# Two-layer graph network: turned 32 x 32 blocks exchanged from SBUF to SBUF by sixteen transfers, in place of four stores and a load

## Chip, cores and metric

One NeuronCore of a Trainium2 chip. The metric is the device time of one execution in microseconds, as the median of several runs. Engines are named PE (TensorE), DVE (VectorE), ACT (ScalarE), POOL (GpSimd) and SP (SyncE, which issues most of the DMA transfers); PEld is TensorE's weight load.

## What is computed

50,000 nodes with 256 channels, 12,500 edges. Cut to what matters:

```
h   = relu(layernorm(x))                             # per node
agg = zeros.at[dst].add(relu(h[src] + edge_attr))    # 12,500 edges
g   = (h + agg) @ W1 + b1                            # 256 -> 512
g   = (g - mean) / sqrt(var + eps) * gamma + beta    # over all nodes
y   = relu(g) @ W2 + b2                              # 512 -> 256
x1  = x + h + relu(graph_norms(y))                   # statistics over all nodes
out = x1 + relu(h1 @ W + segment_sum((h1 @ M)[src])) # h1 = relu(layernorm(x1))
```

The change lies in the two matrix products with W1 and W2, which the kernel calls its stage 2.

## The kernel before

The kernel has four stages, each a block of programs for the five engines with semaphores between them. Stage 1 reads x and the edges, and gathers the statistics for the batch norm. Stage 2 forms h + agg, multiplies by W1 and W2 and writes y and x + h to the table `xy_table` in DRAM. Stages 3 and 4 do the graph norms, the second layer, and its edges.

Stage 2 works on groups of 512 nodes: 128 partitions of 4 nodes (`T`), 97 whole groups and a last one of 84 partitions, 98 (`NG`) in all. A group k passes through these steps, each on one engine, each group one step behind the group before:

- SP loads x (`load_rows`, L1011), POOL gathers the sums of the edges into `ar` (`gather`, L1072), ACT forms h in `hr` (`norm`, L1099), DVE adds them in `ar` (`add`, L1196).
- The product needs channels on the partitions, so `ar` (nodes on the partitions) must be transposed. For groups 0, 1 and 97 (`by_tensor`, L919) TensorE does it. For the other 95 groups DVE transposes inside 32 x 32 blocks (`turn_blocks`, L1214) into `blocks`, the memory of `W2s`, which no longer holds a weight. Then the blocks themselves must change places across the partitions: a quadrant q of 32 source partitions (`SQ`, `QUADS` = 4) holds, for each half c of the channels and each destination quadrant b, a run of 128 numbers.
- That exchange goes through a DRAM table `ht_table`: SP stores each source quadrant to it (`store_blocks`, L1037: four transfers of 128 KB), and when all four have landed loads the whole, 512 KB, into `staged` (`load_turned`, L1001), which is the memory of `WM` for even groups and of `W1s` for odd ones.
- ACT rounds the turned group to `tH` (`keep_high`, L1148), DVE takes the rest as `tL` (`keep_low`, L1224). TensorE multiplies W1 in two parts with `tH`, `tL` (`hidden`, L1346: 4 x 6 matmuls), ACT applies batch norm and relu into `r`, ACT and DVE split that into `rH` and `rL`, and TensorE multiplies W2 (`output`, L1360: 4 x 6 matmuls). ACT keeps y (`keep_y`, L1134), DVE takes statistics, SP stores y (`store_y`, L1029) and x + h (`store_rows`, L1021; called xh below).

The order on every engine is written out by hand: a `step(k)` for ACT, DVE and TensorE, a loop for SP. SP's loop (L1056) calls, for each k, `load_turned(k + 2)`, `load_rows(k + 5)`, `store_rows(k + 2)`, `store_y(k - 2)`, `clear_slots(k - 1)`, `store_blocks(k + 3)`, each with its wait in front; SP executes them in this order, and what waits holds up what follows. `load_rows` reuses the buffer of four groups before (`NU` = 4), so it waits until the xh store of that group has landed. `blocks` is a single buffer: DVE's `turn_blocks(k)` waits until the four stores of group k - 1 have landed (L1220), and `store_blocks` waits for the turn. `staged` has two buffers, free when `tL` of the group two before is made. The first eight groups (`KEPT`) stay in SBUF and have no xh and y stores.

Of the kernel before, what the change touches and what calls it, by code (L numbers as in the profile page):

```python
# [5 lines left out]
FP32 = mybir.dt.float32  # L6
# [6 lines left out]
P = 128  # L13
# [7 lines left out]
KC = CH // P  # L21
# [9 lines left out]
SQ = 32  # L31
QUADS = P // SQ
# [18 lines left out]
def is_int(k):  # L51
    return isinstance(k, int)
# [7 lines left out]
def after(eng, sem, count):  # L60

    if not is_int(count) or count > 0:
        eng.wait_ge(sem, count)


def group_shape(k):

    return (LAST, T) if is_int(k) and k == NG - 1 else (P, T)


def columns(k):

    p, n = group_shape(k)
    return p * n


def group_rows(table, k):

    return table[bass.ds(k * GC, columns(k)), :].rearrange("(p t) c -> p t c", t=T)


def group_block(table, k):

    return table[k] if is_int(k) else table[bass.ds(k, 1)].rearrange("a p b n -> (a p) b n")


def xh_part(block):

    return block[:, 0, :].rearrange("p (t c) -> p t c", t=T)


def y_part(block):

    return block[:, 1, :].rearrange("p (c n) -> p c n", c=KC)
# [51 lines left out]
def gnn_kernel(nc, x, src, dst, edge_attr, W1, b1, bn_gamma, bn_beta, W2, b2, ln_w, ln_b,  # L146
# [9 lines left out]
    xy_table = nc.dram_tensor("xy_table", (NG, P, 2, T * CH), FP32, kind="Internal").ap()  # L156
    x1_table = nc.dram_tensor("x1_table", (NODES, CH), FP32, kind="Internal").ap()
    x1d_table = nc.dram_tensor("x1d_table", (ET * P, CH), FP32, kind="Internal").ap()
    ht_table = nc.dram_tensor("ht_table", (2, QUADS, SQ, KC, QUADS, P), FP32, kind="Internal").ap()

    with ExitStack() as ctx:
        def sb(name, shape, dt=FP32, scope=ctx, side="left"):
# [7 lines left out]
        def sem(name):  # L170
            phase.append(nc.alloc_semaphore(name))
            return phase[-1]
# [740 lines left out]
        def stays(k):  # L913
            return is_int(k) and k < KEPT

        def exists(k):
            return 0 <= k < NG

        def by_tensor(k):  # L919

            return k in (0, 1, NG - 1)

        def turns_until(k):

            return {0: 1, 1: 2, NG - 1: 3}[k]

        def blocks_until(k):

            return k - 1

        def exchanges(k):

            return k // 2

        blocks = W2s[:].rearrange("p a b -> p (a b)")
        staged = [WM[:].rearrange("p a b c -> p (a b c)"), W1s[:].rearrange("p a b -> p (a b)")]
# [9 lines left out]
        xh2_done = sem("xh2_done")  # L946
        h2_done = sem("h2_done")
        blocks_made = sem("blocks_made")
        ht_out = [sem(f"ht_out{s}") for s in range(2)]
        ht_in = [sem(f"ht_in{s}") for s in range(2)]  # L950
        t2_made = sem("t2_made")
        th_kept = sem("th_kept")
# [13 lines left out]
        with ExitStack() as scope, nc.Block() as block:  # L966
# [14 lines left out]
            def xbuf(k):  # L981

                return xh_part(xy_kept[:, k, :, :]) if stays(k) else xr[:, k % NU, :, :]

            def ybuf(k):
                return y_part(xy_kept[:, k, :, :]) if stays(k) else yr[:, k % AU, :, :]

            def turned_part(k, c, n):

                if by_tensor(k):  # L990
                    return hT_ps[:, c, 0:n]
                return staged[k % 2][:, c * GC:(c + 1) * GC].rearrange("p (q t n) -> p t q n", q=QUADS, t=T)

            def nodes_of(part, k):

                return part if by_tensor(k) else part.rearrange("p (t q n) -> p t q n", q=QUADS, t=T)

            @block.sync
            def _(sp):

                def load_turned(k):  # L1001
                    if not exists(k) or by_tensor(k):
                        return
                    if k == 3:
                        sp.wait_ge(q_made, 1)
                    sp.wait_ge(ht_out[k % 2], 16 * QUADS * exchanges(k))
                    after(sp, tl_kept, k - 1)
                    sp.dma_start(staged[k % 2], ht_table[k % 2].rearrange("b p c q n -> (b p) (c q n)")
                                 ).then_inc(ht_in[k % 2], 16)

                def load_rows(k):  # L1011
                    if not exists(k):
                        return
                    p, n = group_shape(k)
                    if k < KEPT + NU:
                        after(sp, h2n_done, k - NU + 1)
                    else:
                        sp.wait_ge(xh_out[k % NU], 16 * (k // NU - KEPT // NU))
                    sp.dma_start(xbuf(k)[0:p, 0:n, :], group_rows(x, k)).then_inc(x2_in[k % NU], 16)

                def store_rows(k):  # L1021
                    if not exists(k) or stays(k):
                        return
                    p, n = group_shape(k)
                    sp.wait_ge(xh2_done, k + 1)
                    sp.dma_start(xh_part(group_block(xy_table, k))[0:p, 0:n, :],
                                 xbuf(k)[0:p, 0:n, :]).then_inc(xh_out[k % NU], 16)

                def store_y(k):  # L1029
                    if not exists(k) or stays(k):  # L1030
                        return
                    n = columns(k)
                    sp.wait_ge(y_kept, k + 1)
                    sp.dma_start(y_part(group_block(xy_table, k))[:, :, 0:n],
                                 ybuf(k)[:, :, 0:n]).then_inc(y_out[k % AU], 16)

                def store_blocks(k):  # L1037
                    if not exists(k) or by_tensor(k):
                        return
                    sp.wait_ge(blocks_made, blocks_until(k))  # L1040
                    after(sp, ht_in[k % 2], 16 * (exchanges(k) - 1))
                    for q in range(QUADS):
                        sp.dma_start(ht_table[k % 2, :, :, :, q, :].rearrange("b p c n -> p c b n"),
                                     blocks[q * SQ:(q + 1) * SQ, :].rearrange("p (c b n) -> p c b n", c=KC, b=QUADS)
                                     ).then_inc(ht_out[k % 2], 16)

                def clear_slots(t):
                    if not 0 <= t < ET:
                        return
                    if t == 0:  # L1050
                        sp.wait_ge(blank_made, 1)
                    sp.dma_start(x1d_table[t * P:(t + 1) * P, :], blank[:]).then_inc(slots_clear, 16)

                for k in range(3):
                    load_rows(k)
                for k in range(-2, NG + 3):  # L1056
                    load_turned(k + 2)
                    load_rows(k + 5)
                    store_rows(k + 2)
                    store_y(k - 2)  # L1060
                    clear_slots(k - 1)
                    store_blocks(k + 3)
                sp.wait_ge(slots_clear, 16 * ET)
                for s in range(AU):
                    sp.wait_ge(y_out[s], 16 * (-(-(NG - s) // AU) - KEPT // AU))
                for s in range(NU):
                    sp.wait_ge(xh_out[s], 16 * (-(-(NG - s) // NU) - KEPT // NU))
# [30 lines left out]
            def _(act):  # L1098
# [49 lines left out]
                def keep_high(k):  # L1148
                    if not exists(k):
                        return  # L1150
                    n = columns(k)
                    if by_tensor(k):
                        act.wait_ge(t2_made, turns_until(k))
                    else:
                        act.wait_ge(ht_in[k % 2], 16 * exchanges(k))
                    after(act, z_made, (k - 1) * HC)
                    for c in range(KC):
                        last = act.activation(nodes_of(tH[:, k % 2, c, 0:n], k), turned_part(k, c, n), ACT.Copy)
                    last.then_inc(th_kept, 1)
# [25 lines left out]
                act.wait_ge(var_made, 1)  # L1185
                act.activation(small[:, 4, :], small[:, 3, :], ACT.Sqrt, bias=eps[:]).then_inc(sdev_made, 1)
                keep_high(0)
                for piece in norm(2):
                    piece()
# [5 lines left out]
            def _(dve):  # L1195
# [18 lines left out]
                def turn_blocks(k):  # L1214

                    if not exists(k) or by_tensor(k):
                        return
                    dve.wait_ge(h2_done, k + 1)
                    if k > 2:
                        dve.wait_ge(ht_out[(k - 1) % 2], 16 * QUADS * exchanges(k - 1))  # L1220
                    dve.transpose(blocks.rearrange("p (b t n) -> p t b n", b=KC * QUADS, t=T),  # L1221
                                  ar[:, k % AU, :, :].rearrange("p t (b n) -> p t b n", n=SQ)).then_inc(blocks_made, 1)

# [99 lines left out]
                residual(2)  # L1323
                add(2)
                turn_blocks(2)
                for k in range(NG + 2):
                    step(k)
# [770 lines left out]
```

## Time and profile before

| | |
|---|---|
| runs | 2348.55 us median of 3 (2345.96 to 2351.61) |
| profiled execution | 2350.93 us, its span 2349.2 us |
| PE busy in the span | 2269.6 us (97%) |
| DVE busy | 1953.0 us (83%) |
| ACT busy | 1832.8 us (78%) |
| POOL busy | 1399.4 us (60%) |
| stage 2 | about 460 to 1545 us of the span |
| queue of the transfers that SP issues | 559.53 MB, 69.4% of 16 DMA engines' time |

The span runs from the first to the last instruction of the one execution that the profiler recorded. Busy time says how long an engine was at work, not that it set the pace; that is read stage by stage, from what waits for what. TensorE's matmuls overlap in the record, so their durations add up to more than the time they take; the number of matmuls in a stretch is the better measure of pace. A line number (L1043) is that of the listing above.

### The profile page before, as it was taken

To read this page: it belongs to the slowest core of one execution; us is meant where nothing else is said; L and a number is where in the kernel's file an instruction comes from. 1 tells how busy PE (TensorE), PEld (TensorE's weight loads), DVE (VectorE), ACT (ScalarE), POOL (GpSimd) and SP (SyncE) were. 2 spreads that over 40 slices of the span, in tenths; PEclk is the share of its full clock that TensorE was granted. 3 is DMA by queue.
4 is the path that set the end of the run, shared out by engine and by line. 5 is a ranking of instruction groups with operands and counts; after the bars stand their busy time and mean duration, and the time that the engine had idled before them with its cause. 6 is when DMAs were issued, how large, how long until landed. Compare 5 with 4: busy or idle time off the path is not lost. (4 is left out here: it accounts for less than half of the span.)

```text
span 2349.2 us, 45141 instructions
## 1 busy us (share of the span) xinstructions
PE 2269.6 (97%) x11499; PEld 1933.4 (82%) x11499; DVE 1953.0 (83%) x5704; ACT 1832.8 (78%) x3645; POOL 1399.4 (60%) x1403
## 2 busy tenths in 40 slices
PE   7999999699999999999999999979999999999997
PEld 6888888478888888788888788859988888989997
DVE  8999998488888888888888888767777777779996
ACT  6999999477777777877777877758888888866664
POOL 5777777464444444445444444237777777777775
PEclk8999999799999999999999999989999999999999
DMA  7899897367878888878877888679999999775662
GB/s 251 279 278 280 271 281 216 105 196 216 255 253 262 262 259 249 269 249 268 260 246 255 268 252 259 214 293 402 410 412 412 414 412 410 298 235 162 172 178 99
DMA packets 360084, 632.17 MB, mean 269 GB/s; under 512 B 61456, under 2 KB 246057, under 8 KB 348482
## 3 DMA queue, kind: packets, MB, share of 16 engines
q1 hardware_dynamic: 300018, 559.53, 69.4%
q0 software_dynamic: 59808, 70.24, 10.3%
q8 instruction: 81, 1.33, 0.2%
q14 instruction: 129, 1.06, 0.1%
q10 hardware_dynamic: 48, 0.01, 0.0%
HBM read 390.04 MB, written 336.65 MB: 309 GB/s over the span
## 5 line engine op out<-in xcount | busy, mean ns | idle before, releaser
L1087 POOL DMA_INDIRECT ar<-sum_table,ids x392 | 409.7, 1045 | 177.9 <-issue 96.2
L1655 POOL DMA_INDIRECT x1d_table<-x1r,slot x392 | 382.5, 976 | 141.7 <-issue 126.1
L1123 ACT ACTIVATE r<-pair,bnC,bnA 128x512 f32<-128x512 f32 x392 | 302.2, 771 | 90.6 <-PE pair L1356 80.0
L2021 PE MATMUL pair<-WM,h1T 128*128 128x256 f32 x1568 | 358.9, 382 | 3.9 <-DVE orr L1847 3.1
L2021 PEld LDWEIGHTS pair<-WM,h1T 128*128 128x128 f32 x1568 | 289.5, 189 | 49.2 <-issue 10.5
L1083 POOL MEMSET ar<- 128x1024 f32 x98 | 93.9, 958 | 386.9 <-DVE W2s L1221 366.2
L835 PE MATMUL bank<-hr 128*128 128x257 f32 (+1 forms) x1568 | 274.3, 329 | 9.3 <-ACT hr L536 9.2
L835 PEld LDWEIGHTS bank<-hr 128*128 128x128 f32 x1568 | 250.9, 192 | 36.8 <-ACT hr L536 9.9
L1268 DVE TENSOR_TENSOR rL<-r,rH 128x512 fp32r<-128x512 f32 x392 | 265.9, 679 | 11.3 <-ACT rH L1132 3.7
L1356 PE MATMUL pair<-tH,W1h 128*128 128x512 f32 (+1 forms) x784 | 242.8, 391 | 8.4 <-DVE tL L1230 8.4
L1356 PE MATMUL pair<-tH,W1l 128*128 128x512 f32 (+1 forms) x784 | 241.8, 390 | 0.0
L1356 PE MATMUL pair<-tL,W1h 128*128 128x512 f32 (+1 forms) x784 | 241.5, 389 | 0.0
L1847 DVE SCALAR_TENSOR_TENSOR orr<-pair,x1r 128x1024 f32<-128x1024 f32 x98 | 120.0, 1225 | 130.6 <-DMA out<-orr 84.5
L1736 ACT ACTIVATE h1r<-x1r,n,r 128x256 f32<-128x256 f32 x392 | 202.6, 593 | 0.0
L536 ACT ACTIVATE hr<-xr,nmr,rstd 128x256 f32<-128x256 f32 x392 | 202.4, 587 | 0.3 <-PE bank L835 0.2
L1109 ACT ACTIVATE hr<-xr,nmr,rstd 128x256 f32<-128x256 f32 x360 | 194.7, 589 | 0.0
L1356 PEld LDWEIGHTS pair<-tH,W1h 128*128 128x128 f32 x784 | 146.9, 188 | 41.8 <-DVE tL L1230 11.7
L1356 PEld LDWEIGHTS pair<-tL,W1h 128*128 128x128 f32 x784 | 147.6, 188 | 30.6
L1356 PEld LDWEIGHTS pair<-tH,W1l 128*128 128x128 f32 x784 | 147.6, 188 | 30.6
L1257 DVE CAST rH<-r 128x512 fp32r<-128x512 f32 x196 | 84.3, 430 | 102.0 <-ACT r L1123 101.8
L1221 DVE STREAM_TRANSPOSE W2s<-ar 128x1024 f32<-128x1024 f32 x95 | 118.3, 1245 | 51.8 <-DMA ht_table<-W2s 50.6
L1372 PE MATMUL pair<-rH,W2h 128*128 128x512 f32 x392 | 153.0, 390 | 0.0
(254 smaller groups left out, 5723.7 us busy)
## 6 DMA issues: line engine op xcount, KB each, us to landing
xr<-in_x SPq DMA_DIRECT2D x186, 512.0 KB, 5.9
xy_kept<-xy_table SPq DMA_DIRECT2D x57, 1024.0 KB, 20.5
x_table<-x1r SPq DMA_DIRECT2D x97, 512.0 KB, 19.9
out<-orr SPq DMA_DIRECT2D x97, 512.0 KB
ht_table<-W2s SPq DMA_DIRECT2D x380, 128.0 KB
xy_table<-xr SPq DMA_DIRECT2D x89, 512.0 KB, 6.6
xy_table<-yr SPq DMA_DIRECT2D x89, 512.0 KB, 7.5
xyr<-xy_table SPq DMA_DIRECT2D x32, 1024.0 KB, 20.1
```

The costliest lines, as they stand in the source:

```text
L536: last = act.activation(hr[0:p, h, j, 0:CH], xr[0:p, s, j, :], ACT.Relu, bias=nmr[0:p, bass.ds(k * T + j, 1)], scale=rstd[0:p, bass.ds(k * ...
L835: return pe.matmul(o, a, b, start=False, stop=False, skip_group_check=True)
L1087: pool.indirect_dma_start(ar[0:p, s, j, :], None, sum_table[:, :], bass.IndirectOffsetOnAxis(ap=ids[0:p, k * T + j:k * T + j + 1], axis=0) ...
L1109: one = act.activation(hr[0:p, k % AU, j, :], xbuf(k)[0:p, j, :], ACT.Relu, bias=nmr[0:p, k * T + j:k * T + j + 1], scale=rstd[0:p, k * T ...
L1123: act.activation(r32[:, m, 0:n], z_ps[m][:, 0:n], ACT.Relu, bias=bnC[:, m:m + 1], scale=bnA[:, m:m + 1]).then_inc(r_kept, 1)
L1268: dve.tensor_tensor(rL[:, k % 2, m, 0:n], r32[:, m, 0:n], rH[:, k % 2, m, 0:n].bitcast(FP32), ALU.subtract).then_inc(rl_kept, 1)
L1356: last = pe.matmul(z_ps[m][:, 0:n], w[:, c, m * P:(m + 1) * P], t[:, k % 2, c, 0:n], start=i == 0, stop=i == len(parts) - 1)
L1372: last = pe.matmul(y_ps[k % 2][c][:, 0:n], w[:, m, c * P:(c + 1) * P], t[:, k % 2, m, 0:n], start=m == 0 and i == 0, stop=m == HC - 1 and ...
L1655: pool.indirect_dma_start(x1d_table[:, :], bass.IndirectOffsetOnAxis(ap=slot[0:p, part, s * T + j:s * T + j + 1], axis=0), x1r[0:p, s, j, ...
L1736: last = act.activation(h1r[0:p, f, j, :], x1r[0:p, s, j, :], ACT.Relu, bias=n3[0:p, s, j:j + 1], scale=r3[0:p, s, j:j + 1])
L1847: dve.scalar_tensor_tensor(out=flat(orr[:, s, :, :], p, n), in0=flat(u_pair(k)[:, :, :], p, n), scalar=0.0, in1=flat(x1r[:, b, :, :], p, n ...
L2021: last = pe.matmul(tile_of(u_pair(k), j)[0:p, :], h1T[:, s, c, j * p:j * p + p], Ws[:, c, :], start=c == 0, stop=c == KC - 1)
```

## The change

The table `ht_table` and its semaphores `ht_out` go. `load_turned` and `store_blocks` are replaced by `exchange`, sixteen transfers from `blocks` to `staged`: for each source quadrant q and destination quadrant b, 32 partitions x 2 runs of 128 numbers, 32 KB. The waits are those of the functions that it replaces: the turn must be made, and `staged` free. ACT's `keep_high` and DVE's `turn_blocks` wait for all sixteen. In SP's loop `load_rows(k + 5)` now stands first.

```
-                def load_turned(k):
+                def exchange(k):
                     if not exists(k) or by_tensor(k):
                         return
-                    if k == 3:
+                    if exchanges(k) == 1:
                         sp.wait_ge(q_made, 1)
-                    sp.wait_ge(ht_out[k % 2], 16 * QUADS * exchanges(k))
+                    sp.wait_ge(blocks_made, blocks_until(k))
                     after(sp, tl_kept, k - 1)
-                    sp.dma_start(staged[k % 2], ht_table[k % 2].rearrange("b p c q n -> (b p) (c q n)")
-                                 ).then_inc(ht_in[k % 2], 16)
+                    for q in range(QUADS):
+                        here = blocks[q * SQ:(q + 1) * SQ, :].rearrange("p (c b n) -> p c b n", c=KC, b=QUADS)
+                        for b in range(QUADS):
+                            there = staged[k % 2][b * SQ:(b + 1) * SQ, :].rearrange(
+                                "p (c q n) -> p c q n", c=KC, q=QUADS)
+                            sp.dma_start(there[:, :, q, :], here[:, :, b, :]).then_inc(ht_in[k % 2], 16)
...
-                def store_blocks(k):
-                    if not exists(k) or by_tensor(k):
-                        return
-                    sp.wait_ge(blocks_made, blocks_until(k))
-                    after(sp, ht_in[k % 2], 16 * (exchanges(k) - 1))
-                    for q in range(QUADS):
-                        sp.dma_start(ht_table[k % 2, :, :, :, q, :].rearrange("b p c n -> p c b n"),
-                                     blocks[q * SQ:(q + 1) * SQ, :].rearrange("p (c b n) -> p c b n", c=KC, b=QUADS)
-                                     ).then_inc(ht_out[k % 2], 16)
...
                 for k in range(-2, NG + 3):
-                    load_turned(k + 2)
                     load_rows(k + 5)
+                    exchange(k + 2)
                     store_rows(k + 2)
                     store_y(k - 2)
                     clear_slots(k - 1)
-                    store_blocks(k + 3)
...
-                        act.wait_ge(ht_in[k % 2], 16 * exchanges(k))
+                        act.wait_ge(ht_in[k % 2], 16 * QUADS * QUADS * exchanges(k))
...
-                        dve.wait_ge(ht_out[(k - 1) % 2], 16 * QUADS * exchanges(k - 1))
+                        dve.wait_ge(ht_in[(k - 1) % 2], 16 * QUADS * QUADS * exchanges(k - 1))
```

On SP, in the middle of stage 2, one round of the loop and the start of the next read so before (L1043 are the four stores, `W2s` is `blocks`; `WM` and `W1s` are the two `staged`; L1019 loads x, L1026 stores xh, L1034 stores y, L1052 clears rows of a table of stage 3):

```order
L1008 DMA WM<-ht_table 128x1024
L1019 DMA xr2<-in_x 128x1024
L1026 DMA xy_table<-xr2 128x1024
L1034 DMA xy_table<-yr 128x1024
L1052 DMA x1d_table<-blank 128x256
L1043 DMA ht_table<-W2s 64x4x128 x4
L1008 DMA W1s<-ht_table 128x1024
```

and so with the change (its lines are numbered anew: L1011 is the exchange, L1021 loads x, L1028 stores xh, L1036 stores y, L1044 clears):

```order
L1021 DMA xr2<-in_x 128x1024
L1011 DMA WM<-W2s 32x2x128 x16
L1028 DMA xy_table<-xr2 128x1024
L1036 DMA xy_table<-yr 128x1024
L1044 DMA x1d_table<-blank 128x256
L1021 DMA xr2<-in_x 128x1024
L1011 DMA W1s<-W2s 32x2x128 x16
```

The load from the table, which stood between the clear and the load of x, is gone, and the exchange stands between the load of x and the xh store. The other four engines have as many instructions as before, in the same order.

## Rows read from the trace of the kernel before

**Rows 1.** Windows of 100 us in stage 2; (x) is the number of instructions.

```profile
core 0: us, PE busy (x) PEld busy (x) DVE busy (x) ACT busy (x) POOL busy (x), PEclk, DMA share, GB/s
...
860.00:960.00 100.00, 98.62 (x434) 80.95 (x433) 82.62 (x116) 76.24 (x126) 45.40 (x45) 1.00 0.81 255
...
1060.00:1160.00 100.00, 100.00 (x443) 82.81 (x442) 85.02 (x120) 77.92 (x130) 47.93 (x47) 1.00 0.82 260
1160.00:1260.00 100.00, 99.32 (x437) 81.54 (x437) 83.29 (x117) 75.79 (x127) 45.71 (x46) 1.00 0.80 257
1260.00:1360.00 100.00, 98.06 (x433) 80.79 (x432) 84.41 (x119) 77.23 (x130) 46.79 (x47) 1.00 0.82 260
```

**Rows 2.** Waits, 470 to 1540 us: who waited for whom, us, times, longest.

```profile
ACT tH L1158 <- DMA WM<-ht_table: 54.5, 33, 4.4
DVE W2s L1221 <- DMA ht_table<-W2s: 50.6, 63, 2.5
ACT tH L1158 <- DMA W1s<-ht_table: 46.6, 30, 2.9
...
PE pair L1356 <- DVE tL L1230: 8.4, 6, 4.3
...
SPq L1008 <- DMA ht_table<-W2s: 371.3, 94, 6.8
```

**Rows 3.** One step in order of time: start, us, engine, line [idle before].

```profile
1001.40 0.33 SPq L1008 DMA_DIRECT2D WM<-ht_table  x1
1001.47 1.25 DVE L1221 STREAM_TRANSPOSE W2s<-ar 128x1024 f32<-128x1024 f32 x1 [1.81 <-DMA ht_table<-W2s]
1001.77 0.43 SPq L1019 DMA_DIRECT2D xr<-in_x  x1
1002.24 0.43 SPq L1026 DMA_DIRECT2D xy_table<-xr  x1
1002.72 0.43 SPq L1034 DMA_DIRECT2D xy_table<-yr  x1
...
1003.92 3.62 SPq L1043 DMA_DIRECT2D ht_table<-W2s  x4
...
1012.39 0.33 SPq L1008 DMA_DIRECT2D W1s<-ht_table  x1
1012.47 1.25 DVE L1221 STREAM_TRANSPOSE W2s<-ar 128x1024 f32<-128x1024 f32 x1 [0.71 <-DMA ht_table<-W2s]
...
1016.29 1.16 ACT L1158 ACTIVATE tH<-W1s 128x512 fp32r<-128x512 f32 x2 [1.81 <-DMA W1s<-ht_table]
```

**Rows 4.** Issues: four stores early, the stores of 560 to 1460 us, ACT's small loads.

```profile
478.40 2.55 SPq L1043 DMA_DIRECT2D ht_table<-W2s  x4
...
L1043 SPq DMA_DIRECT2D ht_table<-W2s x328: 575/869/2428, 562.6 to 1458.6; - x164
...
34.99 0.27 ACTq L590 DMA_DIRECT2D vec_rows<-in_L_gnn_ln_w  x1
35.30 0.28 ACTq L590 DMA_DIRECT2D vec_rows<-in_L_gnn_ln_b  x1
```

**Rows 5.** Issue and landing: a y store alone, then the xh stores of 560 to 1460.

```profile
L1034 SPq DMA_DIRECT2D xy_table<-yr x1: 319/319/319, 1517.1 to 1517.1; - x1
DMA to landing us min/median/max: 2.6/2.6/2.6
...
L1026 SPq DMA_DIRECT2D xy_table<-xr x81: 320/430/1412, 569.1 to 1452.6; - x81
DMA to landing us min/median/max: 5.8/6.6/7.4
```

**Rows 6.** The start of stage 2 in order of time.

```profile
470.19 2.70 SPq L1043 DMA_DIRECT2D ht_table<-W2s  x4
...
473.35 1.22 PE L1356 MATMUL pair<-tH,W1h 128*128 128x512 f32 x2 [4.29 <-DVE tL L1230]
...
475.24 0.33 SPq L1008 DMA_DIRECT2D WM<-ht_table  x1
```

More of the change, by code:

```diff
@@ L158, in gnn_kernel @@
     x1d_table = nc.dram_tensor("x1d_table", (ET * P, CH), FP32, kind="Internal").ap()
-    ht_table = nc.dram_tensor("ht_table", (2, QUADS, SQ, KC, QUADS, P), FP32, kind="Internal").ap()
     with ExitStack() as ctx:
@@ L948, in gnn_kernel @@
         blocks_made = sem("blocks_made")
-        ht_out = [sem(f"ht_out{s}") for s in range(2)]
         ht_in = [sem(f"ht_in{s}") for s in range(2)]
```

## Prediction

> **What bounds the kernel now.** I read the page first, then stage 2 (about 460 to 1545 us) in windows of 100 us, then the waits of that stage, then one step in order of time. The windows say who sets the pace: between 1060 and 1160 us TensorE is busy for 100.00 of 100 us and runs 443 matmuls [rows 1]. That is 100 / 443 = 0.2257 us a matmul; a group takes 48 of them (24 hidden, 24 output), so a step lasts 48 x 0.2257 = 10.83 us. VectorE (85.02) and ScalarE (77.92) have room in the same row. The page has 0.9 to 1.0 for TensorE's clock through these slices, so nothing is to be had there.
>
> What the table route costs is read from the windows that are not full: 434, 437 and 433 matmuls instead of 443 [rows 1], 9 + 6 + 10 = 25 too few, 25 x 0.2257 = 5.6 us. The waits name the cause: TensorE waits for `tL` [rows 2], which waits for `tH`, which waits for the load from the table (54.5 us for `WM` alone). The whole TensorE wait of the stage is 8.4 us [rows 2], but 4.29 us of it is one wait at 473 us [rows 6], for the `tL` of group 1, which TensorE turns and which never goes through the table.
>
> The other waits in rows 2 (VectorE 50.6 us for the stores, SyncE 371.3 us at the load) are off the path; the reader should see that they are nearly on it. In one step [rows 3] SyncE issues the load at 1001.40 and the next one at 1012.39: a round of 10.99 us, of which 1003.92 + 3.62 - 1001.40 = 6.14 us is issuing and 4.85 us is waiting for the stores to land. VectorE's next turn starts 0.08 us after that landing. So the route has a loop as long as TensorE's step, without reserve, and an unlucky transfer now and then makes TensorE wait.
>
> **What is removed and added.** Per group of the 95 that are exchanged, five issues (four stores, one load) go and sixteen come: SyncE goes from 9 to 20 issues a step, 1045 more in all. 512 KB written to DRAM and 512 KB read back become 512 KB from SBUF to SBUF, in 512-byte pieces as the stores had. No other engine gets another instruction. Two waits change: VectorE's turn waits for the exchange of the group before instead of its four stores, ScalarE's `tH` for the exchange instead of the load.
>
> **Price of one issue.** No row shows a 32 x 2 x 128 transfer. From below: small loads of a few rows on ScalarE's queue follow each other in 35.30 - 34.99 = 0.31 us [rows 4]. From above: the 128 KB stores, 2.55 / 4 = 0.64 us each with little ahead of them, and 0.87 us in the median of the full steps, where more stands in the queue [rows 4]. Between them stand the 128 x 1024 transfers, back to back 1002.24 - 1001.77 = 0.47 us [rows 3]. I take **0.40 us**: the new transfer has 64 pieces, between the few rows at 0.31 and the 128 rows at 0.47, and both sides have the same simple shape, unlike the stores. Sixteen: 6.4 us (5.0 at 0.31, 7.5 at 0.47, 10.2 at 0.64, 13.9 at 0.87). These are estimates from the rows named.
>
> **The loop on SyncE.** The new order is load x (k+5), exchange (k+2), store xh (k+2), store y, clear. The load of x waits until the store of xh of the step before has landed (the buffer of four steps ago). In the old order the wait for the stores stood between these two and hid the landing; now only the y store and the clear do. So a round is at least 0.47 (load of x) + 6.4 (exchange) + the landing of the xh store. Alone, a 512 KB store lands 2.6 us after its issue [rows 5]; in the old step the xh store takes 6.6 us, queued behind two 512 KB loads [rows 5]. In the new order it stands behind small transfers that come no faster than they are issued, so I take 3.1 us, near the lower end. Sum: 0.47 + 6.4 + 3.1 = **10.0 us**, 0.8 us inside the step of 10.83. Bounds: 0.47 + 5.0 + 2.6 = 8.1 and 0.47 + 13.9 + 6.6 = 21.0; I stay near the lower, since one 512 KB load stands ahead of the exchange and not the four transfers of rows 3.
>
> **The loop on VectorE.** Turn 1.25 us [rows 3], fifteen issues 6.0, the last transfer 2.0 to land (an estimate, below the 2.6 of a 512 KB store), 0.1 for signals: 9.4 us, also inside the step. The four 128 KB stores show that transfers overlap: issued from 470.19, all landed by 475.24 [rows 6], 5.05 us, not four times 2.6.
>
> **What that does to the chain.** Old: turn ends at 1001.47 + 1.25 = 1002.72, `tH` of that group starts at 1016.29 [rows 3], 13.6 us. New: 6.0 + 2.0 + 0.1 = 8.1 us after the turn. The 5.5 us saved become cushion before TensorE, so the 5.6 us of holes in rows 1 should close. If that cushion is gone, the holes come back. VectorE's 50.6 us and ScalarE's 101 us of waits go too, and turn into waiting for TensorE: nothing is gained there. At the start, the second exchange waits longer than its stores did (8 us against 5.05), so the turns of groups 3 and 4 come 1 to 2 us later; of TensorE's six waits for `tL` [rows 2] the one at 473 us is the only one in the start, and it comes before any exchange has landed, so I cost this at nothing; the step in hand between a turn and its use covers it. Stages 1, 3 and 4 are untouched.
>
> **Sum.** The profiled execution took 2350.93 us (span 2349.2 and 1.7 around it): 2350.93 - 5.6 = 2345.3. It is 2.4 us above the median of the three runs, 2348.55; part of the holes may be this execution's own, so against the median the gain is 2 to 5.6 us. I forecast **2345 us**, -0.15%, below the 0.2% (4.7 us) that a measurement of this kernel can tell from no change. Its own range: 2340 to 2349.
>
> **A rule that speaks against it.** The rows: 128 KB stores are issued 0.64 us apart, and the few-row loads 0.31 [rows 4], so a quarter of the bytes costs more than a quarter of the time: sixteen issues at 0.40 take 6.4 us where four take 2.55. The Trainium skill, "SBUF — State Buffer", section "The DMA setup-cost knee", asks for 128 partitions and the largest single transfer, since each pays a roughly fixed 2 us; sixteen in turn would be an estimated 32 us by that figure, three steps. Rows 6 disagree with the serial reading, since the four stores overlap. What the rows leave of it is the price of an issue, in rivals 1 and 2.
>
> **Rivals.**
> 1. *SyncE becomes the bound* (slower). Place: the wait of load x for the xh store. It decides as soon as sixteen issues and the landing exceed 10.83 - 0.47 = 10.36 us. With 0.47 us an issue and 3.1 us landing the round is 0.47 + 7.5 + 3.1 = 11.1, 0.25 us over; some 88 rounds have both (groups from 8 on store xh), +22 us: about 2370. With 0.50 us and 3.1 it is 11.6, +68 us, about 2415. For it: the reserve of 0.8 us is smaller than the step from 0.40 to 0.47 us an issue makes, 1.1 us. Against: 64 pieces a transfer are fewer than any 0.47 row has. Chance 25%.
> 2. *A small transfer holds the queue as long as a large one.* At the store's 0.64 us: 0.47 + 10.2 + 3.1 = 13.8, 3.0 us over, x 88 = +264 us, about 2610. Were they even to land in turn, 2.6 us each as in rows 5, a round would be 42 us and the stage nearly 3 ms longer, but rows 6 show four that overlap. Against: the 0.31 us row. Chance 7%, of which 1 for the serial case.
> 3. *The holes stay.* If TensorE's three holes come from slow stretches of the DMA engines that hit the exchange as well, nothing moves: 2348.5. Against: rows 2 tie them to the loads, and the route gains 5.5 us of cushion. Chance 8%.
>
> **How the numbers follow.** Forecast 60%, rivals 25, 7 and 8%. Of the forecast's 60%, some 25 points lie at 2344 and below (faster by over 0.2%), 35 within. Rival 3 (8) is within, and about 5 points of rival 1 (an overshoot under 0.05 us a round). Faster 25%, same 48%, slower 27%. For 8 in 10 the range takes the forecast, rival 3 and rival 1 up to 0.3 us over a round (0.3 x 88 = 26 us): 2340 to 2375. Left out are rival 2, the dearer part of rival 1, and a gain beyond 8.5 us, for which rows 1 have no room.
>
> **What the profile will show.** Right: no TensorE wait for `tL` between 560 and 1460 us and 443 matmuls in each full window; sixteen issues in 6 to 7 us; the wait of the turn for the exchange near zero; SyncE waiting for the turn, not for the xh store; DMA share down from about 0.8. Wrong, rival 1: SyncE's largest wait stands at the load of x, for the xh store's landing, and windows of 100 us hold fewer than 440 matmuls throughout. Rival 2: the issues are 0.6 us or more. A faster time than 2340 would mean that TensorE's 0.2257 us itself depended on the transfers.

## The result, and the profile after

The changed kernel takes **2621.11 us**, the median of three runs (2619.4 to 2623.92), against 2348.55: a ratio of 1.1155, 95% interval 1.1138 to 1.1172. It is slower by some 272 us. Forecast were 2345 us, with a range to 2375.

The changed kernel's page: the span, the busy time of the engines, and the queue of the transfers that SP issues.

```profile
span 2619.4 us, 46093 instructions
PE 2356.1 (90%) x11499; PEld 1949.0 (74%) x11499; DVE 1938.8 (74%) x5704; ACT 1830.5 (70%) x3645; POOL 1415.4 (54%) x1403
q1 hardware_dynamic: 304578, 509.79, 55.0%
```

The queue moves 50 MB less and its share falls from 69.4 to 55.0%, as the change meant it to. No engine has a larger share of the span for it. Windows of 100 us, with the columns of [rows 1]:

```profile
960.00:1060.00 100.00, 87.36 (x349) 67.77 (x349) 63.96 (x91) 60.38 (x100) 36.55 (x35) 0.95 0.50 165
1060.00:1160.00 100.00, 83.00 (x348) 63.80 (x347) 66.08 (x94) 61.41 (x103) 37.29 (x36) 1.00 0.52 173
...
1260.00:1360.00 100.00, 82.69 (x346) 63.40 (x344) 66.99 (x97) 61.72 (x103) 40.23 (x38) 1.00 0.51 166
```

These windows have 346 to 349 matmuls where [rows 1] had 433 to 443, and all twelve from 560 to 1760 us lie between 340 and 354. So this is no matter of single holes: 48 x 100 / 348 = 13.8 us a step, in all of stage 2. The same is read from VectorE's turns, whose line gives the start of the first and the last of 95 (first of the kernel before, then of the change):

```profile
L1221 DVE STREAM_TRANSPOSE W2s<-ar x95: 1245/1245/1248, 468.9 to 1494.6; 128x1024 f32<-128x1024 f32 x95
```

```profile
L1212 DVE STREAM_TRANSPOSE W2s<-ar x95: 1245/1245/1248, 468.5 to 1769.2; 128x1024 f32<-128x1024 f32 x95
```

The distance grew from 1025.7 to 1300.7 us, by 275 us: the whole loss lies between these two turns. Divided by 94 it is a mean round of 10.91 us before and 13.84 us after. I use this mean round for the experiments too.

What takes 13.8 us is seen in SP's issues in order of time (start, us, line), with VectorE's two turns beside them:

```profile
1004.95 1.25 DVE L1212 STREAM_TRANSPOSE W2s<-ar 128x1024 f32<-128x1024 f32 x1 [4.32 <-DMA WM<-W2s]
1006.51 0.33 SPq L1021 DMA_DIRECT2D xr<-in_x  x1
1006.94 10.18 SPq L1011 DMA_DIRECT2D W1s<-W2s  x16
1017.17 0.58 SPq L1028 DMA_DIRECT2D xy_table<-xr  x1
...
1018.52 1.25 DVE L1212 STREAM_TRANSPOSE W2s<-ar 128x1024 f32<-128x1024 f32 x1 [4.37 <-DMA W1s<-W2s]
1020.02 0.33 SPq L1021 DMA_DIRECT2D xr<-in_x  x1
```

From one load of x to the next are 13.51 us: 0.43 to the first issue of the exchange, 10.23 for the sixteen (10.18 and a gap), and 1020.02 - 1017.17 = 2.85 us from the xh store to the next load of x, which waits for its landing. Most of the 2.85 us goes on issuing the xh store, the y store and the clear; the wait that is left is 93.5 / 86 = 1.1 us a round (SP's line among the waits below). Each of the sixteen takes 10.23 / 16 = **0.64 us**. The lines of the exchange (into `W1s`; that into `WM` is alike) and of the xh store (min/median/max ns of an issue, first and last start) and the landing of the latter:

```profile
L1011 SPq DMA_DIRECT2D W1s<-W2s x752: 585/597/1934, 483.1 to 1767.2; - x188
...
L1028 SPq DMA_DIRECT2D xy_table<-xr x90: 575/584/1412, 560.0 to 1782.6; - x90
...
DMA to landing us min/median/max: 2.8/2.9/3.7
```

An issue lasts 597 ns in the median and follows the one before by some 40 ns more; a few take up to 1.9 us, which brings the mean round from 13.51 to 13.84. Last the waits of the stage, and SP's own:

```profile
DVE W2s L1212 <- DMA W1s<-W2s: 221.6, 47, 6.0
DVE W2s L1212 <- DMA WM<-W2s: 216.1, 47, 5.8
PE pair L1347 <- DVE tL L1221: 157.6, 95, 4.1
ACT tH L1149 <- DMA W1s<-W2s: 112.5, 47, 3.6
...
SPq L1021 <- DMA xy_table<-xr: 93.5, 86, 1.8
```

Against [rows 2] TensorE now waits for `tL` at each of the 95 groups (157.6 us where it was 8.4), the turn waits 437.7 us in all for the exchange, and SP's largest wait stands at the load of x: the place that the prediction named for rival 1, with the price of rival 2.

### The profile page after: what moved, and what is told of

Its sections match the earlier page's. It is cut to its first block and busy times, and to the rows that moved or that the text cites. A ratio compares the mean times of both kernels' runs of the same rounds, so it can differ in the third digit from the quotient of the medians.

```text
span 2619.4 us, 46093 instructions
## 1 busy us (share of the span) xinstructions
PE 2356.1 (90%) x11499; PEld 1949.0 (74%) x11499; DVE 1938.8 (74%) x5704; ACT 1830.5 (70%) x3645; POOL 1415.4 (54%) x1403
## 5 line engine op out<-in xcount | busy, mean ns | idle before, releaser
L1078 POOL DMA_INDIRECT ar<-sum_table,ids x392 | 427.4, 1090 | 177.9 <-issue 96.3
L1347 PE MATMUL pair<-tH,W1h 128*128 128x512 f32 (+1 forms) x784 | 257.1, 410 | 157.6 <-DVE tL L1221 157.6
L1347 PE MATMUL pair<-tL,W1h 128*128 128x512 f32 (+1 forms) x784 | 250.4, 402 | 0.0
L1347 PE MATMUL pair<-tH,W1l 128*128 128x512 f32 (+1 forms) x784 | 247.8, 398 | 0.0
L1363 PE MATMUL bank<-rH,W2h 128*128 128x512 f32 (+1 forms) x392 | 159.3, 406 | 24.5 <-DVE rL L1259 24.5
L1363 PE MATMUL pair<-rH,W2h 128*128 128x512 f32 x392 | 164.3, 419 | 13.1 <-DVE rL L1259 12.7
```

The lines of the kernel that those rows point to most:

```text
L1078: pool.indirect_dma_start(ar[0:p, s, j, :], None, sum_table[:, :], bass.IndirectOffsetOnAxis(ap=ids[0:p, k * T + j:k * T + j + 1], axis=0) ...
L1347: last = pe.matmul(z_ps[m][:, 0:n], w[:, c, m * P:(m + 1) * P], t[:, k % 2, c, 0:n], start=i == 0, stop=i == len(parts) - 1)
L1363: last = pe.matmul(y_ps[k % 2][c][:, 0:n], w[:, m, c * P:(c + 1) * P], t[:, k % 2, m, 0:n], start=m == 0 and i == 0, stop=m == HC - 1 and ...
```

## The experiments

Five of the kernels, e1, e2, e3, e5 and e11, were run once each. In e1, e2, e5 and e11 blocks land in other places or not at all: they serve to time transfers, and are no kernels to use. A ratio is taken to runs of the kernel before on the same chip, whose median is 2349.85 us for e1 to e4, 2351.6 for e5 to e7 and 2353.9 for e8 to e11.

### e1_shapes: is it the shape of the transfer?

The sixteen transfers of a group take nine shapes, by ranges of groups; two of them:

```
-                    for q in range(QUADS):
...
+                        elif k < 45:
+                            sp.dma_start(there[:, i * 64:i * 64 + 64],
+                                         blocks[:, i * 64:i * 64 + 64]).then_inc(inc, 16)
...
+                        elif k < 75:
+                            h, w = i % 8 * 16, i // 8 * 512
+                            sp.dma_start(there[h:h + 16, w:w + 512],
+                                         blocks[112 - h:128 - h, w:w + 512]).then_inc(inc, 16)
```

> The sixteen transfers of an exchange get nine shapes, each for some ten groups (31 to 13 in turn); the blocks land in other places or not at all, so the output is not the reference's. Shapes: 32x2x128 (as in the change), 32x256, 32x128 (half the bytes), 128x64, 128x2x32, 64x128, 16x512, 32x8x32, 128x32 (half the bytes). Theory 1, a price per issue: SyncE pays about 0.64 us for each, whatever it carries, in all nine; rounds of 13.5 us throughout. Theory 2, the bytes: the queue is held by moving 512-byte pieces from SBUF to SBUF, so the halved shapes 32x128 and 128x32 go down to about 0.32 us and their rounds to TensorE's 10.8 us, the rest stays at 0.64. Theory 3, the shape: transfers of 128 partitions cost 0.33 to 0.47 us as the 128x1024 ones do in the kernel before, those of 32 partitions 0.64; or the number of pieces decides, then 32x8x32 and 128x2x32 (256 pieces) are dearest and 16x512 cheapest.

It took 2622.25 us. Three of the nine lines of issues, in order 32 x 128 (half the bytes), 128 x 2 x 32 (four times the pieces) and 16 x 512:

```profile
L1017 SPq DMA_DIRECT2D W1s<-W2s x80: 512/591/1552, 785.9 to 904.8; - x80
...
L1023 SPq DMA_DIRECT2D W1s<-W2s x80: 600/621/1539, 1061.8 to 1186.7; - x80
...
L1031 SPq DMA_DIRECT2D W1s<-W2s x80: 507/589/1429, 1342.4 to 1462.5; - x80
```

All nine medians lie between 589 and 621 ns. From SBUF to SBUF, bytes (16 or 32 KB), pieces and partitions hardly matter: the price is one of the issue, and the time of the kernel does not move.

### e2_eight: half as many issues

Eight transfers of 64 partitions x 2 x 128 in place of sixteen of 32, with the same 512 KB in all:

```
+                    for i in range(8):
+                        h, w = i % 2 * 64, i // 2
+                        here = blocks[64 - h:128 - h, :].rearrange("p (c b n) -> p c b n", c=KC, b=QUADS)
+                        there = staged[k % 2][h:h + 64, :].rearrange("p (c q n) -> p c q n", c=KC, q=QUADS)
+                        sp.dma_start(there[:, :, w, :], here[:, :, w, :]).then_inc(ht_in[k % 2], 16)
```

> The same 512 KB in eight transfers of 64 partitions, 64x2x128, in place of sixteen of 32 (the blocks land in other places, so the output is not the reference's). Theory 1, a price per issue of 0.64 us: 8 x 0.64 = 5.1 us, a round of 0.47 + 5.1 + 2.9 = 8.5 us, below TensorE's 10.83, so the time is about 2345 us. Theory 2, the bytes: as many 512-byte pieces move, the exchange stays at 10.2 us and the time at 2620 us. Theory 3 with pieces or partitions in the price: between 0.64 and 1.28 us an issue; at 1.28 the time stays at 2620.

It took 2341.41 us, beside 2349.85 of the kernel before (median of 7, lowest 2344.18). One round of SP, and a window:

```profile
1006.14 5.14 SPq L1010 DMA_DIRECT2D WM<-W2s  x8
```

```profile
1260.00:1360.00 100.00, 100.00 (x443) 82.80 (x442) 85.16 (x119) 79.11 (x131) 46.10 (x47) 1.00 0.65 210
```

The price is the same, 5.14 / 8 = 0.64 us, and with eight of them the stage runs at TensorE's pace. So the number of issues makes the loss. The holes of [rows 1] are gone as well. This run changes SP's order along with the route, so it does not tell which of the two closes them; e9 below does.

### e3_load_after: the exchange ahead of the load of x

```
-                    load_rows(k + 5)
                     exchange(k + 2)
+                    load_rows(k + 5)
```

> The change with the load of x behind the exchange, so that SyncE no longer waits for the xh store between two exchanges. If the sixteen issues are the cost (theory 1), the next loop takes over, VectorE's: turn 1.25, signals 0.1, sixteen issues 10.2, landing 1.4: 13.0 us in place of 13.5, 88 x 0.5 = 44 us less, about 2577 us. If the order of the loop is the cost (the wait of the load of x for the xh store), the time falls to 2345 us.

2638.95 us, slower than the change. SP in order of time:

```profile
1011.11 10.97 SPq L1011 DMA_DIRECT2D W1s<-W2s  x16
1022.12 0.58 SPq L1021 DMA_DIRECT2D xr<-in_x  x1
...
1024.89 5.26 SPq L1011 DMA_DIRECT2D WM<-W2s  x7
```

The wait for the xh store is gone, and SP issues from end to end: 1024.89 - 1011.11 = 13.78 us, sixteen issues now 11.01 us (1022.12 - 1011.11). A round of 13.0 us was expected, VectorE's loop. It did not come, since the sixteen take 0.8 us more, most of it at their first, as a window that ends behind it shows; VectorE's turn of that round stands beside it:

```profile
1011.11 1.21 SPq L1011 DMA_DIRECT2D W1s<-W2s  x1
```

```profile
1023.46 1.25 DVE L1212 STREAM_TRANSPOSE W2s<-ar 128x1024 f32<-128x1024 f32 x1 [4.61 <-DMA W1s<-W2s]
```

VectorE's loop grows by the same time: its turn ends at 1023.46 + 1.25 = 1024.71, 0.18 us before the next exchange, so here the loops on SP and on VectorE are equally long. The order of the load of x alone is not the cost.

### e5_ends: does the price hang on the two ends?

The sixteen transfers go between other ends, by ranges of groups, by way of two tables in DRAM made for it (`probe`, strided, and `probe_flat`, one run of 32 KB a transfer):

```
+                        elif k < 35:
+                            sp.dma_start(there[b * SQ:(b + 1) * SQ, :].rearrange("p (c q n) -> p c q n", c=KC, q=QUADS)[:, :, q, :],
+                                         probe[k % 2, b, :, :, q, :]).then_inc(inc, 16)
+                        elif k < 45:
+                            sp.dma_start(there[b * SQ:(b + 1) * SQ, q * 256:q * 256 + 256],
+                                         flat.rearrange("(p n) -> p n", p=SQ)).then_inc(inc, 16)
...
+                        elif k < 65:
+                            sp.dma_start(there[b * SQ:b * SQ + 2, q * 256:q * 256 + 128],
+                                         flat[0:256].rearrange("(p n) -> p n", p=2)).then_inc(inc, 16)
+                        elif k < 75:
+                            sp.dma_start(there[b * SQ:b * SQ + 2, q * 256:q * 256 + 128],
+                                         blocks[q * SQ:q * SQ + 2, b * 256:b * 256 + 128]).then_inc(inc, 16)
```

> The sixteen transfers of an exchange get other ends and sizes, each for some ten groups (the blocks don't reach their places, so the output is not the reference's): groups 2 to 5 as in the change, then SBUF to DRAM 32x2x128 and 32x256, DRAM to SBUF 32x2x128, 32x256 and 128x64, DRAM to SBUF 2x128, SBUF to SBUF 2x128, DRAM to DRAM 32x256, SBUF to DRAM 128x64. Theory A, SBUF at both ends is what costs 0.60 us: those with an end in DRAM are issued in 0.31 to 0.47 us. Theory B, every transfer on SyncE's queue costs 0.60 us when it directly follows another of its kind, whatever its ends, and only transfers of a few rows cost the 0.31 us that the prediction took as its lower bound: 2x128 at 0.3, the others at 0.60. Theory C, the 0.31 us belongs to ScalarE's queue: 2x128 costs 0.60 here too.

It took 2455.48 us. The lines of issues, in order: SBUF to strided DRAM, strided DRAM to SBUF, contiguous DRAM to SBUF, two rows of 512 bytes from DRAM to SBUF, two such rows from SBUF to SBUF, DRAM to DRAM:

```profile
L1017 SPq DMA_DIRECT2D probe<-W2s x144: 549/595/1559, 519.6 to 638.3; - x144
...
L1023 SPq DMA_DIRECT2D W1s<-probe x80: 544/594/1711, 752.7 to 873.5; - x80
...
L1026 SPq DMA_DIRECT2D W1s<-probe_flat x80: 398/421/1178, 891.8 to 986.0; - x80
...
L1032 SPq DMA_DIRECT2D W1s<-probe_flat x80: 246/253/431, 1113.4 to 1200.1; - x80
...
L1035 SPq DMA_DIRECT2D W1s<-W2s x80: 562/563/698, 1217.4 to 1330.3; - x80
...
L1038 SPq DMA_DIRECT2D probe_flat<-probe_flat x160: 473/589/1671, 1346.9 to 1479.3; - x160
```

An issue lasts 0.42 us where one end is a contiguous run in DRAM, and 0.59 to 0.60 us where both are in SBUF, both in DRAM, or the one in DRAM is strided in pieces of 512 bytes (some 0.04 us more to the next issue in each case). Even a kilobyte from SBUF to SBUF costs 0.56 us, where the same kilobyte from DRAM costs 0.25. That last is also on SP's queue, so the 0.31 us of ScalarE's small loads [rows 4] was no property of ScalarE's queue. A stride by itself is not what costs: the xh and y stores write 4 KB pieces to every other 4 KB of `xy_table`, in 0.43 us [rows 3]. Why the chip does so, these rows do not say.

Nor is the price the transfer's alone. The xh store, the same throughout, stands right behind the sixteen; first behind those to strided DRAM, then behind those from contiguous DRAM:

```profile
569.49 0.58 SPq L1059 DMA_DIRECT2D xy_table<-xr  x1
...
899.21 0.42 SPq L1059 DMA_DIRECT2D xy_table<-xr  x1
```

In both it takes as long as each of those ahead of it, and in the change 584 ns (the L1028 line above) where it had 430 [rows 5]. Behind the two rows from SBUF to SBUF it takes less than they do, 0.40.

### e7_act_six: six of the sixteen on ScalarE's queue

```
-                    for q in range(QUADS):
...
+                    for q, b in moves[6:]:
+                        move(sp, k, q, b)
...
                     high(k, 0)
+                    part(k + 2, 0)
                     keep_high(k + 1)
-                    for piece in pieces[0:2]:
...
+                    part(k + 2, 1)
```

Here `move` is the transfer of the change, and `part(k, i)` the i-th of them issued by ScalarE, behind one of its activations.

> The sixteen transfers of the change, six of them issued on ScalarE's queue, one behind each of six activations, and ten on SyncE's. If the price is one queue's own and ScalarE's issues hide beside its activations: ten issues 6.4 us, VectorE's loop 1.25 + 0.1 + 6.5 + 1.4 = 9.3 us, SyncE's 0.47 + 6.4 + 2.9 = 9.8 us, both inside TensorE's 10.83: 2341 to 2350 us. If an issue holds ScalarE for 0.6 us: 8.5 + 3.6 = 12.1 us a step, about 2470 us. If both queues share one generator, sixteen issues still take 10.2 us: 2600 us.

2348.76 us (2344.14 to 2352.06), a ratio of 0.9985 to the kernel before (0.9972 to 0.9997). Part of a step:

```profile
1004.82 6.83 SPq L1002 DMA_DIRECT2D W1s<-W2s  x10
...
1007.22 0.60 ACTq L1002 DMA_DIRECT2D W1s<-W2s  x1
1007.92 0.63 ACT L1153 ACTIVATE tH<-WM 128x512 fp32r<-128x512 f32 x1
1007.97 0.60 ACTq L1002 DMA_DIRECT2D W1s<-W2s  x1
```

The same sixteen transfers through the same 16 DMA engines: 272 us of loss are gone, and the windows from 560 to 1460 us hold 442 or 443 matmuls. So it is not on the DMA engines that the sixteen hold each other up; what they use up is the time of the engine that issues, or of its queue: this run moves both, and does not tell them apart. ScalarE's issues last 0.60 us as SP's do, but its activations run on beside them. The Trainium skill, "DMA: Bandwidth & Descriptors", section "Issuing engines are not separate DMA queues", says that issuing from several engines only saves the sequencer's time, which is usually small beside the transfer. The first half fits this run; the second did not hold here, where that time, sixteen times 0.64 us of a step of 10.83, was the bound.

### e4_twelve and e11_twelve_bare: twelve issues

In e4 POOL copies the four blocks that keep their partitions (q = b), and the load of x stands behind the exchange; in e11 the four are left out from group 4 on, and nothing else changes:

```
                         for b in range(QUADS):
+                            if k > 3 and b == q:
+                                continue
```

> Only the twelve blocks that change their quadrant go by transfers; GpSimd copies the four that stay in their partitions (four copies of 32x2x128), and the load of x stands behind the exchange. Theory 1: VectorE's loop is 1.25 + 0.1 + 12 x 0.64 + 1.4 = 10.4 us, SyncE issues 12 x 0.64 + 2.2 = 9.9 us a round, both below TensorE's 10.83: 2345 to 2355 us, level with the kernel before. Were GpSimd's copies to cost over 1.5 us each, or the gathers to come late through them, 2400 us or more.

> The change with twelve transfers for each group from the fifth on: the four blocks that stay in their partitions are left out, so the output is not the reference's. The round measured in the change is 13.52 us; four issues of 0.64 less make 10.96, 0.13 us above TensorE's step of 10.83: 2341 (what eight transfers gave) + 88 x 0.13 = about 2352 us. If something else than the number of issues holds the round, for instance the landing, it stays above 2500 us.

e4 took 2485.98 us, a ratio of 1.0585 (1.0556 to 1.0614). POOL in order of time, twice the same place of its round:

```profile
1006.52 2.71 POOL L1101 COPY W1s<-W2s 32x256 f32<-32x256 f32 x4 [1.58 <-DMA ar<-sum_table,ids]
...
1018.80 2.72 POOL L1101 COPY WM<-W2s 32x256 f32<-32x256 f32 x4 [1.66 <-DMA ar<-sum_table,ids]
```

A round of 12.28 us, the second of the two cases expected: with four copies, and the wait for its gathers that they need, POOL became the loop. That answered nothing on SP, so e11 left the blocks out: 2393.38 us, where 2352 was worked out. SP in order of time:

```profile
1007.65 0.33 SPq L1023 DMA_DIRECT2D xr<-in_x  x1
1008.08 7.62 SPq L1013 DMA_DIRECT2D W1s<-W2s  x12
...
1018.62 0.33 SPq L1023 DMA_DIRECT2D xr<-in_x  x1
```

This round is 10.97 us, as worked out. But the mean from the first to the last turn is 11.38 (470.3 to 1540.0 us): single issues of up to 1.9 us are never made up where the loop has no reserve. An undisturbed round is a lower bound.

### e6_one_store, e9_stores_first, e8_one_store_first: the table route, in other orders

The e5 prices suggested another route through the table: one contiguous store of 128 x 1024 and four strided loads (e6, in the order of the kernel before):

```
+                    sp.dma_start(ht_table[k % 2], blocks).then_inc(ht_out[k % 2], 16)
...
+                    for b in range(QUADS):
+                        sp.dma_start(staged[k % 2][b * SQ:(b + 1) * SQ, :].rearrange("p (c q n) -> p c q n", c=KC, q=QUADS),
+                                     there[b]).then_inc(ht_in[k % 2], 16)
```

e9 is the kernel before with SP's order alone changed, the stores first; e8 is e6 in this order:

```
-                    load_turned(k + 2)
+                    store_blocks(k + 2)
                     load_rows(k + 5)
+                    load_turned(k + 2)
                     store_rows(k + 2)
                     store_y(k - 2)
                     clear_slots(k - 1)
-                    store_blocks(k + 3)
```

> The table route of the kernel before with the permutation moved from the store to the load: one store of 128x1024, and four loads of 32 partitions, five issues a group as before. The buffer of the blocks is free when one store has landed (2.9 us) instead of four (8.5 us), and the group is back after 2.9 + 4 x 0.64 + 2 = 7.5 us instead of 13.6. If TensorE's holes come from the length of the route: no TensorE wait for tL after the start, about 2341 us as with eight transfers, -0.35%. If they come from something else, 2349 us. If loads of 512-byte pieces from DRAM are slow (over 8 us for four), slower than before.

> The kernel before with SyncE's order alone changed: the four stores to the table, the load of x, the load from the table, the store of xh, the store of y, the clear. Its stores no longer stand behind the x, xh, y and clear transfers of the same round. If the route was long because of what stood ahead of it in the queue: stores landed some 5 us after the turn (as at the start of the stage, 5.05 us) instead of 9.7, no waits of TensorE for tL after the start, 2341 us, -0.4%. If the route itself is long: 2349 us or more.

> One store and four loads again, now with the order of the stores-first kernel: store to the table, load of x, four loads from the table, xh, y, clear. If its 3% loss came from the store landing behind three 512 KB transfers (6.2 us): now about 2.9 us, and the time is 2341 us. If it came from the four loads: 2430 us again.

| | us, median (runs) | ratio to the kernel before | mean round, us |
|---|---|---|---|
| e6 | 2430.45 (2415.41 to 2430.99) | 1.0321 (1.0284 to 1.0359) | 11.73 |
| e9 | 2343.33 (2342.11 to 2345.22) | 0.9952 (0.9939 to 0.9964) | 10.82 |
| e8 | 2341.98 (2339.7 to 2346.57) | 0.9951 (0.9937 to 0.9965) | 10.81 |

The expectation for e6 was wrong. SP in order of time in e6, and then in e8:

```profile
1006.31 1.33 SPq L1044 DMA_DIRECT2D ht_table<-W2s  x1
1012.56 2.53 SPq L1010 DMA_DIRECT2D WM<-ht_table  x4
```

```profile
1006.59 0.32 SPq L1044 DMA_DIRECT2D ht_table<-W2s  x1
1006.95 0.43 SPq L1021 DMA_DIRECT2D xr<-in_x  x1
1009.46 2.53 SPq L1010 DMA_DIRECT2D WM<-ht_table  x4
```

The same store, for whose landing the loads wait, is through 6.25 us after its issue begins where the load of x, the stores of xh and y and the clear stand ahead of it, and 2.87 us after where it goes first. In e6 the next store must wait for that landing and for SP's 5.4 us of issues (1006.31 - 1000.88, where the loads before began): 5.43 + 6.25 = 11.68 us, 0.85 over the step. In e8 the store has gone before the rest is issued, and the round falls to TensorE's. In e9 the same order does it for the four stores of the kernel before. A window of e9:

```profile
1260.00:1360.00 100.00, 100.00 (x443) 82.81 (x442) 86.18 (x121) 78.86 (x130) 45.68 (x47) 1.00 0.86 263
```

443 where [rows 1] had 433 in this window, with all the traffic through DRAM still there and the DMA share at 0.86: the holes came from the place of the route in SP's queue, not from its bytes.

### e10_act_later: the exchange on two queues, with a later start

In e7 TensorE lost 7.4 us in one wait that ended at 479.6 us, as ScalarE waited for the turn of group 2; 4.3 us of it stands in the kernel before too [rows 6]. In e10 SP issues all sixteen of that group:

```
+                    for q, b in moves[ACT_MOVES if k > 2 else 0:]:
...
+                    if not exists(k) or by_tensor(k) or k == 2:
```

> Six transfers on ScalarE's queue again, but all sixteen of the first exchanged group on SyncE's, so that ScalarE does not wait for the turn at the start of the stage. The run before had 443 matmuls in every full window and lost 7.4 us at 479 us: 2341 to 2343 us if that was all it lost, 2349 if not.

2345.3 us (2343.82 to 2348.99), a ratio of 0.9962 (0.995 to 0.9975): the route of the change, faster than the kernels before and after the change, but not the 2341 to 2343 expected. The start still loses, now at the turn of group 3:

```profile
ACT tH L1153 <- DVE W2s L1234: 6.4, 1, 6.4
```

Both kernels with issues on ScalarE have such a wait: the window of 460 to 560 us holds 379 matmuls in e7, 383 in e10, 411 in e8. The best versions are e8 and e9; the intervals do not tell them apart, and that of e10 overlaps both.

## Why the prediction was wrong, step by step

- **What bounds the kernel now**: right. TensorE's 0.2257 us a matmul is the floor in every run that comes near it (442 or 443 matmuls in each full window of e2, e7, e8, e9 and e10).
- **Price of one issue**: the step that failed. It said 0.40 us; the issues follow each other at 0.64. The number of pieces was the wrong scale: by e1 it makes next to no difference, by e5 the ends do, and what stands ahead in the queue has a share. The lower row, 0.31 us, was a few-row load out of DRAM, and the 0.47 us came from 128 x 1024 transfers with one end in DRAM. The only row in [rows 4] with strided ends was the four stores at 2.55 / 4 = 0.64, which was exactly the price; the reason given for leaving it, that both sides of the new transfer have the same simple shape, had no row behind it.
- **The loop on SyncE**: right in its form, wrong in one term. It was 0.47 + 6.4 + 3.1 = 10.0; measured are 0.43 + 10.23 + 2.85 = 13.51. The load of x and the landing of the xh store (2.9 us in the median, no longer the 6.6 of [rows 5]) came as said. The whole error is the 3.8 us of the sixteen issues. With 13.51 against a step of 10.83 no cushion was left to close anything.
- **The loop on VectorE**: said 9.4 us, with fifteen issues at 6.0. With the measured 0.64 us it would be 1.25 + 9.6 + 2.0 + 0.1 = 13.0 us, over the step as well. In e3, which was to show it as the next bound, it is as long as SP's loop (13.8 us), so it was never seen on its own.
- **What that does to the chain**: not reached in the change. In e2 the holes are closed, as said; but e9 closes them with the table kept, by SP's order alone, so it was not the detour through DRAM as such that made them, but its place in SP's queue. Their size was too low. 5.6 us were read from three windows; from the first to the last turn the kernel before takes 1025.7 us, e9 1017.1 and e8 1016.4, so 8.6 to 9.3 us are to be had there.
- **Rival 1** had the right place and the right point of decision (10.36 us for issues and landing; measured 13.1). **Rival 2** had the right price: 0.64 us, a round of 13.8, 2610 us. It got 7% where [rows 4] held its number. Its words, a small transfer that holds the queue as long as a large one, came out as well: by e1 and e2 the price hardly depends on the size. The serial case in it did not come: the sixteen land 2.0 us after the last of them is issued (the turn at 1018.52 against 1016.53). **Rival 3** falls with e2 and e9. The serial reading worked out from the Trainium skill, "SBUF — State Buffer", section "The DMA setup-cost knee", sixteen times 2 us in turn and an estimated 32 us a round, did not come either: the trace has 13.5.
- **What the profile will show**: the signs named for rivals 1 and 2 are the ones that appeared, and they sufficed to place the cause.

## What to carry to other kernels

Count the issues of each queue per step, and price each by a row whose two ends lie as the new transfer's ends do; from SBUF to SBUF, bytes between 1 and 32 KB and pieces said little here. Where a queue is near the length of a step, one small transfer more per step is worth its whole issue, and fewer, larger ones or a second engine's queue give it back. What others wait for goes first in the queue: moving four stores ahead (e9) gained 10.6 us by the medians, no less than the exchange without the table in eight transfers (e2, 8.4 us in one run).

## What the runs showed of the hardware that was not expected

- **The ends set the price of an issue, and what stands ahead of it has a share**: 0.25 to 0.62 us on the same queue, with the numbers under e1 and e5. The cause stays open.
- **A wait on SP can be nearly free.** In e3 the sixteen issues took 11.01 us, with the wait of the change 10.23. Most of the difference stands at the first of them, 1.21 us above, and 1.27 in the median of the rounds against 0.59 in the change; from the third on they last 0.60 in both. In e3 it is issued right behind the load of x, the xh and y stores and the clear, in the change behind a wait and one load. What holds it there is open.
- **TensorE's clock halves in the changed kernel**, behind some of its waits. Windows of the change (PEclk is the third number from the right), behind a wait of TensorE of 1.88 us that ends at 999.55:

```profile
998.00:1000.00 2.00, 0.45 (x2) 0.41 (x3) 2.00 (x4) 0.97 (x2) 1.46 (x2) 1.00 0.27 68
...
1001.00:1002.00 1.00, 1.00 (x4) 0.76 (x3) 0.00 (x0) 0.23 (x1) 0.00 (x0) 0.50 0.25 66
...
1004.00:1006.00 2.00, 2.00 (x10) 1.65 (x9) 1.05 (x1) 1.13 (x3) 0.00 (x0) 1.00 0.75 297
```

The granted clock goes from 2.4 to 1.2 GHz and back. The wait alone does not explain it: eleven waits of 1.84 to 1.88 us for `tL` stand between 1040 and 1181 us, where the clock stays at 1.00. It costs the kernel nothing: the window from 1060 us has 1.00 throughout and 348 matmuls, the one from 960 us has 0.95 and 349, since SP's round is the longer one.
